# A two-layer kernel on one core: setup and the last quarter of g reordered, and 24 idle transposes at the start

## The reference

```
mod = (silu(c) @ wmod).reshape(32, 6, 1, 256)      # sa, ca, ga, sb, cb, gb
ga, gb = sign * max(|.|, 0.25)
h = layernorm(x) * (1 + ca) + sa
# attention part: a scan over tokens, a matrix, and a convolution of 5 taps per channel
s_t = a * s_(t-1) + (1 - a) * h_t
x = x + ga * (s @ W^T + b + conv5(h) + conv_b)
# FFN part: each row picks one of 8 experts by its last token
h = layernorm(x) * (1 + cb) + sb
sel = argmax(softmax(gelu(h_last @ Wp1 + bp1) @ Wp2 + bp2))
r = gelu(h @ W1[sel] + b1[sel]) @ W2[sel] + b2[sel]
x = x + gb * (h + 0.3 * (r @ Wo + bo))
```

## Time and profile before

| what | value |
|---|---|
| median of 3 runs | 730.27 us (730.19 to 731.02) |
| the profiled execution | 731.28 us |
| its span | 729.5 us |
| busy: PE, DVE, ACT, POOL | 91%, 83%, 78%, 64% of the span |
| first `up` matmul | 103.66 us |
| one row in the steady state | some 19.7 us |
| instructions | 11394 |

### The profile page before, as it was taken

The page is one execution under the profiler, slowest core; times in us unless marked ns, Lnnn a source line. Parts: engine busy times, 40 slices in busy tenths (PEclk is TensorE's granted clock), DMA queues, the critical chain, the costliest instruction groups (busy, mean ns, idle before and its releaser), DMA issues.

```text
span 729.5 us, 11394 instructions
## 1 busy us (share of the span) xinstructions
PE 666.3 (91%) x3431; PEld 516.4 (71%) x3431; DVE 603.6 (83%) x1350; ACT 569.8 (78%) x978; POOL 467.3 (64%) x432
## 2 busy tenths in 40 slices
PE   4777839999999999999999999999999999999986
PEld 1666627777777777777777777777777777777764
DVE  1577656999999999999999999999999999997721
ACT  3556828888888888888888889888888888888663
POOL 2552417777666667676777766666667767776542
PEclk9997969999999999999999999999999999999999
DMA  9968073555444545545455544545555455544451
GB/s 295 306 213 293 7 223 117 174 172 157 136 152 154 161 168 174 164 155 173 153 168 174 166 143 138 172 141 165 174 172 153 168 161 158 173 145 134 130 171 59
DMA packets 55457, 120.60 MB, mean 165 GB/s; under 512 B 5643, under 2 KB 43364, under 8 KB 46180
## 3 DMA queue, kind: packets, MB, share of 16 engines
q1 hardware_dynamic: 50260, 114.07, 49.5%
q10 hardware_dynamic: 5136, 5.80, 2.5%
HBM read 61.12 MB, written 25.19 MB: 118 GB/s over the span
## 4 chain that ended last, share of the span: by engine, by line
DVE 45%; POOL 19%; PE 17%; issue 10%; DMA 5%; ACT 3%; ACTq 0%; POOLq 0%; DVEq 0%; SPq 0%
DVE Y L731 26%; POOL g_lo L424 9%; DVE st L681 5%; DVE xr L780 4%; POOL rstd L410 4%; POOL S_lo L432 4%; PE Q L933 3%; DVE nm L688 3%; POOL nmr L412 2%; PE Q L880 2%; DMA xr<-in_L_ffn_W_dram 2%; DVE rT L769 2%; PE Y L897 2%; PE Y L893 2%; DVE mv L685 2%
## 5 line engine op out<-in xcount | busy, mean ns | idle before, releaser
L424 POOL TENSOR_TENSOR g_lo<-g,g_hi 128x512 fp32r<-128x512 f32 x128 | 191.9, 1499 | 177.0 <-ACT g_hi L541 171.7
L731 DVE SCALAR_TENSOR_TENSOR Y<-h,taps,Y 128x512 f32<-128x512 f32 x320 | 222.7, 750 | 4.6 <-PE Y L897 0.2
L534 ACT ACTIVATE g<-U,up_w 128x512 f32<-128x512 f32 x128 | 88.5, 691 | 40.6 <-PE U L915 37.7
L913 PE MATMUL U<-hid_hi,up_w 128*128 128x512 f32 x256 | 107.5, 420 | 13.6 <-DMA up_w<-up_table 13.6
L928 PE MATMUL Q<-g_hi,down_w 128*128 128x512 f32 x256 | 112.8, 441 | 2.3
L502 ACT ACTIVATE S<-xr,nmr,rstd 128x256 f32<-128x256 f32 x128 | 66.7, 593 | 50.5 <-POOL S_lo L432 43.9
L914 PE MATMUL U<-hid_hi,up_w 128*128 128x512 f32 x256 | 101.5, 397 | 0.0
L915 PE MATMUL U<-hid_lo,up_w 128*128 128x512 f32 x256 | 101.5, 396 | 0.0
L929 PE MATMUL Q<-g_hi,down_w 128*128 128x512 f32 x256 | 101.0, 394 | 0.0
L933 PE MATMUL Q<-g_lo,down_w 128*128 128x512 f32 x256 | 87.1, 421 | 14.9 <-POOL g_lo L424 14.9
L432 POOL TENSOR_TENSOR S_lo<-S,S_hi 128x512 fp32r<-128x512 f32 x64 | 82.2, 1286 | 5.0 <-ACT S_hi L642 5.0
(11 more groups left out here) (128 smaller groups left out, 1341.5 us busy)
## 6 DMA issues: line engine op xcount, KB each, us to landing
up_w<-up_table SPq DMA_DIRECT2D x32, 1027.0 KB, 6.7
down_w<-down_tab SPq DMA_DIRECT2D x32, 1024.0 KB, 8.6
xr<-in_L_attn_x_dram SPq DMA_DIRECT2D x32, 512.0 KB, 3.5
out_dram<-xr SPq DMA_DIRECT2D x64, 256.0 KB, 2.3
xr<-in_L_ffn_W_dram ACTq DMA_DIRECT2D x8, 512.0 KB, 8.9
w_raw<-in_L_ffn_W_dram SPq DMA_DIRECT2D x7, 512.0 KB, 6.5
up_table<-down_w SPq DMA_DIRECT2D x2, 1024.0 KB, 11.6
up_table<-up_w SPq DMA_DIRECT2D x2, 1024.0 KB, 8.1
```

The costliest lines, as they stand in the source:

```text
L424: nc.gpsimd.tensor_tensor(g_lo[:, f], g[:, f % 2], g_hi[:, f].bitcast(f32), ALU.subtract).then_inc(g_lo_ready, 1)
L534: nc.scalar.activation(g[:, f % 2], U[f % 2][:, :], ACT.Gelu, bias=up_w[:, i % 2, U_B1 + f:U_B1 + f + 1].bitcast(f32)).then_inc(gelu_out, 1)
L731: ins = nc.vector.scalar_tensor_tensor(out=Y[c][:, :], in0=h[:, c, k:k + T], scalar=taps[:, c, k:k + 1], in1=Y[c][:, :], op0=ALU.mult, op1 ...
L913: mm(U[f % 2][:, :], up_w[:, par, UP + w:UP + w + P], hid_hi[:, par, c], start=(c == 0), stop=False)
```

## The change

Three things are done.

1. In each slot, POOL subtracts g_lo of quarters 2 and 3 one after the other and both S_lo after them; ACT runs gelu and g_hi of quarter 3 between the two S_hi copies.
2. The setup is reordered. SP holds back the loads of W2[0], W, Wo, W1[0], W2[1] and W1[1] until wmod is there (W2[0] and W2[1] are moved to SP for it); each third of wmod has its own semaphore. The modulation rows are transposed before W. DVE scans row 0 right after `mods_setup`, the beta products come behind row 0's transposes, and h waits for an earlier semaphore (`s_mods1`). The casts, subtractions and table writes of W1 have other places, and a Gelu that nobody reads follows the sigmoids, so that the table of the activation is loaded there.
3. TensorE transposes the identity 14 times before and 10 times after the transposition of the vectors, into banks TR, which nobody reads.

```diff
@@ SP @@
             load_x(0)
+            for n in range(NMOD):
+                sp.wait_ge(s_wmod[n], 16 * DC)
+            load_w2(0)
             sp.dma_start(w_nat, ...).then_inc(s_w, 16)
             sp.dma_start(wo[:, :, :], ...).then_inc(s_wo, 16)
             load_w1(0)
+            load_w2(1)
             load_w1(1)
             load_x(1)
...
+            sp.wait_ge(s_modT, 1)
+            load_w1(2)
+            load_x(2)
             sp.wait_ge(s_vec_cols, 1)
...
-            sp.wait_ge(s_modT, 1)
-            load_w1(2)
             load_w1(3)
-            load_x(2)
+            split_out(0)
+            load_w1(4)
+            split_out(1)
+            split_out(2)
             sp.wait_ge(s_beta3, DC)
...
-            load_w1(4)
-            split_out(0)
-            split_out(1)
-            load_w1(5)
-            split_out(2)
-            load_w1(6)
-            split_out(3)
             sp.wait_ge(s_w2T_mm, 4)
             load_x(3)
+            load_w1(5)
+            split_out(3)
+            load_w1(6)
+            split_out(4)
             load_w1(7)
-            for e in range(4, E):
+            for e in range(5, E):
                 split_out(e)
@@ POOL, slot(i) @@
                 if i == -3:
                     w1_lo(0)
-                    w1_lo(1)
+                if i == -1:
+                    w1_lo(5)
...
                 if i == -2:
-                    w1_lo(4)
-                    w1_lo(5)
+                    w1_lo(3)
                 if row(i + 4):
                     norm1(i + 4)
+                if i == -1:
+                    w1_lo(6)
+                    w1_lo(7)
                 if row(i):
                     g_low(i, 2)
+                    g_low(i, 3)
                 if row(i + 3):
                     s_low(i + 3, 0)
-                if row(i):
-                    g_low(i, 3)
-                if row(i + 3):
                     s_low(i + 3, 1)
                 if i == -3:
+                    w1_lo(1)
                     w1_lo(2)
-                    w1_lo(3)
                 if i == -2:
-                    w1_lo(6)
-                if i == -1:
-                    w1_lo(7)
+                    w1_lo(4)
@@ ACT @@
-            load_w2(0)
-            load_w2(1)
...
+            act.wait_ge(s_keep, 1)
+            nc.scalar.activation(nav[:, :], keep[:, 0:1], ACT.Gelu)
...
+            def s_high(r, c):
+                wait(act, mix_done, DC * r)
+                act.wait_ge(S_ready, DC * r + c + 1)
+                nc.scalar.copy(S_hi[:, c], S[:, c]).then_inc(S_hi_ready, 1)
@@ ACT, slot(i) @@
                 if i == -3:
-                    w1_hi(0)
...
-                    w1_hi(1)
                     w2T_copy(0)
-                    (mixT, moved down)
+                    w1_hi(0)
...
                 if i == -2:
-                    w1_hi(4)
+                    w1_hi(3)
+                if i == -1:
                     w1_hi(5)
-                if i == -1:
-                    w1_hi(7)
...
                 for e in experts_at(i, "t3"):
                     expert(e)
+                if i == -1:
+                    w1_hi(6)
+                    w1_hi(7)
...
+                if i == -3:
+                    w2T_copy(1)
+                    (mixT)
                 if row(i + 3):
-                    (S_hi of both halves)
+                    s_high(i + 3, 0)
+                if row(i):
+                    gelu(i, 3)
+                    g_high(i, 3)
+                if row(i + 3):
+                    s_high(i + 3, 1)
+                if i == -3:
+                    down_high(0)
+                    w1_hi(1)
+                    expert(1)
+                    w1_hi(2)
+                else:
+                    for e in experts_at(i, "t1"):
+                        expert(e)
                 if i == -2:
                     gate1(i + 2)
+                    w1_hi(4)
                 if row(i):
-                    gelu(i, 3)
-                    g_high(i, 3)
                     act.wait_ge(gbeta_ready, i + 1)
@@ DVE, slot(-3) @@
                     mods_setup()
+                    scan(0)
+                    (mix_w)
                     dve.wait_ge(s_betaT, 1)
                     (beta3)
-                    (mix_w)
@@ PE @@
+            def warm(n):
+                for k in range(n):
+                    nc.tensor.transpose(TR[k % 2][:, 0:P], ident[:, :], ident[:, :])
+            warm(14)
             pe.wait_ge(s_vecs, VECS_LOADED)
             nc.tensor.transpose(U[1][:, 0:VECS], vec_rows[:, :], ...)
+            warm(10)
             pe.wait_ge(s_silu, DC)
             pe.wait_ge(s_vec_cols, 1)
-            pe.wait_ge(s_wmod, 16 * DC * NMOD)
             for n in range(NMOD):
+                pe.wait_ge(s_wmod[n], 16 * DC)
...
             w2_transposes(0)
+            (transposes of mod_rows, then those of W)
```

More of the change, by code:

```diff
@@ L182, in adaln_attention_ffn_kernel @@
         s_wo = sem("s_wo")
-        s_wmod = sem("s_wmod")
+        s_wmod = [sem(f"s_wmod{n}") for n in range(NMOD)]
         s_small = sem("s_small")
@@ L489, in _ @@
                 for c in range(DC):
-                    act.dma_start(wmod_sb[c][n], wmod[c * P:(c + 1) * P, n * 512:(n + 1) * 512]).then_inc(s_wmod, 16)
-            load_w2(0)
-            load_w2(1)
+                    act.dma_start(wmod_sb[c][n], wmod[c * P:(c + 1) * P, n * 512:(n + 1) * 512]).then_inc(s_wmod[n], 16)
             act.wait_ge(s_cT, 1)
@@ L520, in w2T_copy, with down_high @@
                     load_w2(nxt[0])
-            def expert(e):
-                if e + 1 < E:
-                    w2T_copy(e + 1)
+            def down_high(e):
                 for k in range(2):
@@ L528, in expert @@
                                          scale=OUT_SCALE).then_inc(s_down_hi, 1)
+            def expert(e):
+                if e + 1 < E:
+                    w2T_copy(e + 1)
+                down_high(e)
+            def s_high(r, c):
+                wait(act, mix_done, DC * r)
+                act.wait_ge(S_ready, DC * r + c + 1)
+                nc.scalar.copy(S_hi[:, c], S[:, c]).then_inc(S_hi_ready, 1)
             def gelu(i, f):
@@ L636, in slot @@
                     g_high(i, 2)
-                if row(i + 3):
[L638 to L641, removed]
-                        nc.scalar.copy(S_hi[:, c], S[:, c]).then_inc(S_hi_ready, 1)
-                if i == -2:
-                    w1_hi(6)
-                for e in experts_at(i, "t1"):
-                    expert(e)
-                    if i == -3:
-                        w1_hi(e + 2)
-                if i == -2:
-                    gate1(i + 2)
+                if i == -3:
+                    w2T_copy(1)
+                    act.wait_ge(s_wT, 1)
+                    act.wait_ge(s_fresh, 1)
+                    for c in range(DC):
+                        nc.scalar.activation(mixT[:, c], Y[0][:, c * D:(c + 1) * D], ACT.Copy,
+                                             scale=fresh[:, c:c + 1]).then_inc(s_mixT, 1)
+                if row(i + 3):
+                    s_high(i + 3, 0)
                 if row(i):
@@ L653, in slot @@
                     g_high(i, 3)
+                if row(i + 3):
[8 more added lines that the diff above has]
+                        expert(e)
+                if i == -2:
+                    gate1(i + 2)
+                    w1_hi(4)
+                if row(i):
                     act.wait_ge(gbeta_ready, i + 1)
@@ L792, in slot @@
                     mods_setup()
+                    scan(0)
+                    dve.wait_ge(s_mixT, DC)
+                    nc.vector.tensor_copy(mix_w[:, 0], mixT).then_inc(s_mix_w, 1)
+                    dve.wait_ge(s_mix_w, 1)
+                    nc.vector.tensor_tensor(mix_w[:, 1], mixT, mix_w[:, 0].bitcast(f32), ALU.subtract).then_inc(s_mix_w, 1)
                     dve.wait_ge(s_betaT, 1)
@@ L810, in slot @@
                     nc.vector.max_index(sel8[:, r % 2], top8[:, :], U[1][0:1, 8:8 + E]).then_inc(sel_ready, 1)
-                if row(i + 3):
+                if row(i + 3) and i > -3:
                     scan(i + 3)
@@ L848, in _ @@
             w2_transposes(0)
-            pe.wait_ge(s_mod_rows, 1)
+            for m in range(6 * DC):
+                n, at = m * P // 512, m * P % 512
+                pe.wait_ge(s_mod_rows, n + 1)
+                ins = nc.tensor.transpose(Q[1][:, m * B:(m + 1) * B], mod_rows[n][:, at:at + P], ident[0:B, 0:B])
+            ins.then_inc(s_modT, 1)
             pe.wait_ge(s_w, 16)
@@ L854, in _, with betas @@
             ins.then_inc(s_wT, 1)
-            for m in range(6 * DC):
-                n, at = m * P // 512, m * P % 512
-                pe.wait_ge(s_mod_rows, n + 1)
-                ins = nc.tensor.transpose(Q[1][:, m * B:(m + 1) * B], mod_rows[n][:, at:at + P], ident[0:B, 0:B])
-            ins.then_inc(s_modT, 1)
-            pe.wait_ge(s_wo, 16)
-            b2_view = vecs[:, V_B2:V_B2 + E * DC].rearrange("p (e c) -> p e c", c=DC)
```

(11 more changed lines are left out.)

18 lines of the change are left out of this document (7 added, 11 removed).

## The result

The kernel after takes 710.45 us (median of 4 runs, 710.00 to 711.72) where the kernel before takes 730.45 us in the same session (4 runs, 730.19 to 731.02): a ratio of 0.9728 [0.9711, 0.9745], so 20.0 us or 2.7% less. 706.4 was forecast. The profiled execution of after took 710.11 us, its span is 708.2.

What follows compares the result with a forecast made beforehand. No engine is full; chains of waits bound the setup up to the first up matmul, then a row every 19.68 us. 731.28 - 10.4 (rows) - 13.5 (setup) - 1.0 (to the median) = 706.4; range 700 to 717.

Steps and rivals of the forecast that it cites:

- The row term: Steady rows: new g and S order on POOL and ACT saves 0.36 us in each of 29 slots, 10.4 us.
- the restart: TensorE's low matmuls in the mix: a waited-for matmul delays its successor, taking 0.11 off the 0.47 us slot gain.
- The setup term: Start to first up matmul: reordered loads and setup steps bring it from 103.66 to 90.2, 13.5 us earlier.
- x(0) lands near 8.5: Setup start: row 0's load lands near 8.5 us, so ACT's xn1 is done at 14.1 and modT at 16.0.
- the wait for W2[6]: Setup, expert 6: its load, 15.47 us before, is issued near 44 and has 15 us until TensorE wants it.
- The forecast's case in which the clock does not rise: Modulation matmuls on TensorE's lower clock end at 16.5 us, 2.1 earlier than before instead of 4.9.
- A: Rival: DMA bounds the setup and its lead is lost, leaving 5 of 13.5 us: 714.9; chance 0.15.
- B: Rival: the row keeps its period because DVE or ACT holds conv: 716.8; chance 0.11.
- C: Rival: both terms reach their upper ends, 17 and 13.6 us: 699.7 or a little below; chance 0.07.
- E: Rival: nothing gained, terms cancel or the g order and loads have no effect: 730; chance 0.03.
- D: Rival, slower: DVE's nm misses POOL's pass at the slot's end, conv starts 0.65 later: 735.7; chance 0.04.
- 0.28 short of being the bound: DVE in the row: rT ends near 260.82, 0.28 us before conv's new start at 261.10.

Runs made afterwards that it cites:

- e1: Kernel before with only the new order of the last quarter of g and S on POOL and ACT, setup unchanged: 720.61 us, ratio 0.9853.
- e5: Kernel after without the 24 idle transposes on TensorE: 710.63 us, ratio 0.9719 to before.
- e6: Kernel after with ACT copying the modulation rows ahead of row 0's normalisation instead of behind it: 709.72 us, ratio 0.9708 to before.
- e3: Kernel after with ACT in its old order (both S_hi ahead of gelu 3) and POOL in the new one: 741.09 us, ratio 1.0136 to before.
- e8: Kernel after with the mix's eight high matmuls ahead of its four low ones: 699.24 us, ratio 0.9570 to before.
- e2: Kernel after with the old order of g and S in the rows, new setup and transposes kept: 720.10 us, ratio 0.9850 to before.
- two small edits after this one: Kernel after with the mix's high matmuls first and ACT's normalise waiting for S_lo half by half: 690.00 us, ratio 0.9441 to before.

## Why the prediction was right, and what it mis-sized

The forecast was 706.4, the result 710.45; faster, in the range, and by the two mechanisms named. Where the 4.05 us are:

1. **The row term: 10.4 forecast, 8.7 measured.** The steps (g_lo 3 directly behind g_lo 2, S_lo 1 not moved, g_hi 3 in time, TensorE's wait now put down to S_lo, no wait of 0.59 for Q) all came, and e1 shows the term alone. The gain of a row was 0.313, not 0.36. 0.03 of it is the restart, taken at 0.11: from TensorE's low matmul to ACT's second gelu it is 5.58 us in after (284.84 to 290.42) and 5.44 before (261.07 to 266.51), 0.14. The last 0.02 is not itemised. And the first slot gave nothing (19.86 and 19.85 from the first `up` to its conv): 28 slots, not 29. 10.4 - 8.7 = 1.7.
2. **The setup term: 13.5 forecast, 12.6 measured.** Its sum was nearly right with wrong parts, and that is partly luck: t2(0) was 3.5 late, the last copy of expert 6 2.7, POOL's end 2.0 and the last write 0.9, since the later steps took less than forecast. Failed: "x(0) lands near 8.5" (10.0), hence modT at 16.0 (17.55), the mods setup of 3.0 us (4.4, with the pair held at 19.19), and TensorE's clock, taken as high once it had risen, which was at 0.50 from 19 to 25 and cost some 2.0 on the chain. Right: the wait for W2[6] gone, W1[6] and W1[7] ahead of S_lo(2). Better than forecast: the last write took 5.9 us from POOL's end where 7 were taken, near the 5.58 of a write alone. The forecast's case in which the clock does not rise (2.1 earlier instead of 4.9) was tested by e5: the modulation matmuls end 1.8 us later, and that does not come out at the end. So the clock of these twelve matmuls did not bound this place; ACT did, as the forecast says, and the 24 transposes earned nothing measurable.
3. **From profile to median: 1.0 taken off, but the profile of after lies 0.3 below its median,** so 1.3 of the error is in this step, and 0.1 in what lies around the span. 1.7 + 0.9 + 1.3 + 0.1 = 4.0.

The rivals. A (the lead lost to DMA) did not come as a whole; the nearest to it is ACT's wait of 2.16 us for W1[0] in e6. B is refuted by the period and by e1. C (699.7) and E (730) lie far outside the measured time. D's step exists and did not decide: the ve of norm2 took 1.33 instead of 0.16 in 6 slots of after and in 7 of before, and in after each such slot lasted 0.66 longer and the next 0.67 less; and the slower case came by another way than D, in e3, where ACT was late for POOL. The forecast's words on DVE, "0.28 short of being the bound", were wrong on what DVE's distance was: with nm held 0.7 by hid_lo it had more.

Open: which of the 1 to 2 us differences in the first `up` (90.8 to 93.0 over the runs with the new setup) are the kernel's; x(0) was there between 10.00 and 11.44, the vectors between 6.04 and 7.41. Open also: what TensorE's lower level between 19 and 25 costs at the end, which no run changes alone. And 0.34 of e8's period is only partly itemised: its TensorE still shows 3.2 us of waits for g_lo and 1.3 for rT between 130 and 600 us, 0.18 a row without restarts.

## What to carry to other kernels

Find the engine whose work plus stops makes up the period, and count its stops by the starts of its instructions, each with its restart; the chain of waits may run through another engine for half of its length and still not be what a small shift moves. An order changed on one engine is only worth what the orders of its suppliers allow: half of the row part, on top of the new setup, costs 21 us (e3 against e2), the whole of it gives some 10 (e1). When a stop is only moved, look at once at what could be placed into it: two small edits after this one were worth as much again as the change itself.

## What the runs showed of the hardware

- A DVE instruction of 512 numbers and 0.17 us takes 0.94 when POOL is in a subtraction with two SBUF inputs, and ends with it (252.71 and 252.68); the pair of mods took 2.40 for 0.36, a scan 4.43 for 2.33. The Trainium skill, "SBUF — State Buffer", section "Who interferes with whom", states that a DVE instruction in a two-port mode and a GpSimd one exclude each other for the whole instruction, and that a DVE instruction with two SBUF inputs contends with a GpSimd one that reads SBUF. The trace agrees, and shows it for an instruction this small; whether nm runs in a two-port mode, no row shows. I had priced it only at the slot's end.
- TensorE's clock after a pause: behind 7.29 us of standing the first `up` matmuls of after ran on the lower level from 91.02 to 96.3 (granted clock 0.50), and before, behind 13.62 us, from 103.66 to 108.1 (0.50). In that slot it cost both kernels nearly alike: conv came 19.85 and 19.86 us behind the first `up`.
- A matmul that was waited for is followed 0.33 to 0.34 us later instead of 0.23: a stop costs 0.10 to 0.11 us more than the wait itself, and two stops made into one save that once.
